# A scaled copy on ScalarE in place of a VectorE product in a chunked scan (one Trainium2 core)

## The reference

```python
proj = hidden_states @ in_proj_w.T
gate, xBC, dt = split(proj)
xBC = silu(conv4(xBC))                    # x, B, C
dt = softplus(dt + dt_bias)
A = -exp(A_log)
# per head: a linear recurrence over the tokens
#   y[t] = sum over s <= t of  C[t].B[s] * exp(sum of dt*A over s+1..t) * dt[s] * x[s]
y = ssd(x * dt, dt * A, B, C) + D * x
hg = y * silu(gate)
s = rmsnorm(hg) @ out_proj_w.T
x = x + s * silu(experts(xn))
```

## Time and profile before

| | us |
|---|---|
| median of 3 runs | 546.95 (546.5 to 547.79) |
| the profiled execution | 545.88 |
| its span, first to last instruction | 544.1 |
| PE busy in the span | 465.5 (86%) |
| VectorE busy | 398.3 (73%) |
| ScalarE busy | 177.0 (33%) |
| GpSimd busy | 288.1 (53%) |

### The profile page before, as it was taken

One profiled execution on the slowest core, in us unless ns is written; L12 is line 12 of the kernel. 1 busy time (PEld: TensorE's weight loads), 2 busy tenths in 40 slices (PEclk: granted clock), 3 DMA queues, 4 the chain that ended last, 5 costly groups with the idle time before them and its releaser, 6 DMA issues. The chain is left out here.

```text
span 544.1 us, 7366 instructions
## 1 busy us (share of the span) xinstructions
PE 465.5 (86%) x2270; PEld 338.3 (62%) x2271; DVE 398.3 (73%) x880; ACT 177.0 (33%) x385; POOL 288.1 (53%) x263
## 2 busy tenths in 40 slices
PE   1786677779998999988889999998959999999970
PEld 1772235566877777956576788997426665665650
DVE  5307898999999999998999999996205544544550
ACT  2541632332333323322323323221323434434420
POOL 3100749583678566586265598991025444444440
PEclk9999677987999979999779999987888999999995
DMA  8994210000000000000000000194863232232224
GB/s 273 295 169 53 104 52 1 1 1 11 9 3 11 10 1 10 11 10 11 1 1 11 11 10 12 39 343 155 311 217 106 87 103 81 88 106 78 68 59 173
DMA packets 27176, 42.10 MB, mean 77 GB/s; under 512 B 2980, under 2 KB 19880, under 8 KB 26952
## 3 DMA queue, kind: packets, MB, share of 16 engines
q1 hardware_dynamic: 23432, 30.53, 19.3%
q0 software_dynamic: 3712, 11.17, 6.9%
HBM read 31.42 MB, written 14.47 MB: 84 GB/s over the span
## 5 line engine op out<-in xcount | busy, mean ns | idle before, releaser
L494 POOL TENSOR_TENSOR ARENA<-ARENA 128x512 f32<-128x512 f32 x112 | 143.1, 1314 | 3.7 <-issue 2.5
L836 PEld LDWEIGHTS BANK<-ARENA 128*128 128x128 f32 x768 | 95.3, 204 | 12.4 <-DVE ARENA L1145 6.5
L836 PE MATMUL BANK<-ARENA 128*128 128x64 f32 x768 | 95.9, 287 | 6.5 <-DVE ARENA L1145 6.0
L788 PE MATMUL BANK<-ARENA,W_MAIN 128*128 128x512 f32 x160 | 82.5, 664 | 16.0 <-DVE ARENA L1145 12.5
L900 PE MATMUL BANK<-ARENA 128*128 x184 | 84.6, 603 | 1.7 <-ACT ARENA L708 1.6
L956 DVE TENSOR_TENSOR ARENA<-ARENA 128x256 f32<-128x256 f32 (+9 forms) x110 | 66.2, 602 | 3.3
L788 PEld LDWEIGHTS BANK<-ARENA,W_MAIN 128*128 128x128 f32 x160 | 32.1, 212 | 56.0 <-issue 31.0
L900 PEld LDWEIGHTS BANK<-ARENA 128*128 128x128 f32 x184 | 35.4, 194 | 37.3 <-issue 36.3
L1126 DVE SCALAR_TENSOR_TENSOR ARENA<-BANK,CONVC,ARENA 128x511 f32<-128x511 f32 (+2 forms) x72 | 53.4, 745 | 3.3 <-ACT ARENA L623 1.6
L557 POOL DMA_INDIRECT final_rows<-ARENA x23 | 24.4, 1060 | 54.7 <-DVE ARENA L956 54.7
L956 DVE TENSOR_TENSOR BANK<-BANK,ARENA 128x256 f32<-128x256 f32 (+1 forms) x112 | 51.8, 463 | 0.8
(11 more groups left out here) (130 smaller groups left out, 755.7 us busy)
## 6 DMA issues: line engine op xcount, KB each, us to landing
ARENA<-in_w_gate SPq DMA_DIRECT2D x8, 512.0 KB, 8.4
ARENA<-in_w_up SPq DMA_DIRECT2D x8, 512.0 KB, 9.3
ARENA<-in_w_down SPq DMA_DIRECT2D x8, 512.0 KB, 10.2
ARENA<-x_by_expert SPq DMA_DIRECT2D x23, 129.0 KB, 3.2
mixer_rows<-ARENA SPq DMA_DIRECT2D x16, 128.5 KB, 2.0
ARENA<-in_x SPq DMA_DIRECT2D x4, 512.0 KB, 5.7
mixer_rows<-in_x SPq DMA_DIRECT2D x1, 2048.0 KB
out_dram<-final_rows SPq DMA_DIRECT2D x4, 512.0 KB, 6.1
```

Of the source, the lines that this page charges most:

```text
L494: nc.gpsimd.tensor_tensor(out=XS[par][:, slot, :].rearrange("p (a h) -> p a h", a=HD), in0=E2[par][:, slot, :].unsqueeze(1).to_broadcast([ ...
L788: ins = nc.tensor.matmul(bank[:, :], lhsT=W_MAIN[:, k, i * P:(i + 1) * P], rhs=XNT[:, k, t * GW:(t + 1) * GW], start=(k == 0), stop=(k == ...
L836: ins = nc.tensor.matmul(bank[:, at:at + 64], lhsT=XS[par][:, lev - 1, blk * P:(blk + 1) * P], rhs=odd(GM[par][:, lev - 1, :], lev), start ...
```

## The change

The neighbour weights W1 move from VectorE to ScalarE. GpSimd's E2 product takes all eight slots instead of seven (128x512 for 128x448 elements), so that DT is multiplied into the NEXT slot there, and ScalarE scales that slot by GD in `turn`, in place of VectorE's product in `head`. The E2 product is a function of its own, `decays`, and is issued in `head` of its tile: in GpSimd's queue that is ahead of Y and S1 of the tile before, where it used to be behind them. The waits follow.

```diff
-        E2 = [part(XSLOTS * HEADS).rearrange("p (l h) -> p l h", l=XSLOTS) for _ in range(2)]
+        E2 = [part(SLOTS * HEADS).rearrange("p (l h) -> p l h", l=SLOTS) for _ in range(2)]
...
-            def sources(t):
+            def decays(t):
                 par = t % 2
                 if t > 1:
                     pool.wait_ge(x_scaled, (t - 1) * XSLOTS)
+                    pool.wait_ge(w1_ready, t - 1)
                 pool.wait_ge(a_moved, a_of("pair", t - par, 1))
                 nc.gpsimd.tensor_tensor(
-                    out=E2[par], in0=E[:, 0:XSLOTS, par, :],
-                    in1=heads_of(DT, t).unsqueeze(1).to_broadcast([P, XSLOTS, HEADS]), op=ALU.mult).then_inc(e2_ready, 1)
+                    out=E2[par], in0=E[:, :, par, :],
+                    in1=heads_of(DT, t).unsqueeze(1).to_broadcast([P, SLOTS, HEADS]), op=ALU.mult).then_inc(e2_ready, 1)
+
+            def sources(t):
+                par = t % 2
                 pool.wait_ge(e2_ready, t + 1)
...
-                if kind == "head" and t == 0:
-                    sources(0)
+                if kind == "head":
+                    decays(t)
+                    if t == 0:
+                        sources(0)
...
                     if t > 0:
                         act.wait_ge(e2_ready, t)
-                        act.wait_ge(w1_ready, t)
...
                 if kind == "turn":
+                    act.wait_ge(e2_ready, t + 1)
+                    if t > 1:
+                        act.wait_ge(a_moved, a_of("turn", t - 2, 1))
+                    nc.scalar.activation(W1[par].rearrange("p (r h) -> p r h", r=2),
+                                         E2[par][:, NEXT, :].unsqueeze(1).to_broadcast([P, 2, HEADS]), ACT.Copy,
+                                         scale=GD[par][:, 1:2]).then_inc(w1_ready, 1)
...
                 if kind == "mid":
+                    pe.wait_ge(d_moved, d_of("head", t))
                     for lev in range(1, LEVELS):
...
                         dve.wait_ge(w0_ready, t - 1)
+                        dve.wait_ge(w1_ready, t - 1)
...
-                    dve.wait_ge(gd_ready, (t + 1) * 2)
-                    dve.wait_ge(a_moved, a_of("pair", t - par, 1))
-                    nc.vector.scalar_tensor_tensor(
-                        out=W1[par].rearrange("p (r h) -> p r h", r=2),
-                        in0=E[:, NEXT, par, :].unsqueeze(1).to_broadcast([P, 2, HEADS]), scalar=GD[par][:, 1:2],
-                        in1=heads_of(DT, t).unsqueeze(1).to_broadcast([P, 2, HEADS]),
-                        op0=ALU.mult, op1=ALU.mult).then_inc(w1_ready, 1)
```

## The result

| | before | after |
|---|---|---|
| median of the timed runs, us | 547.21 (10 runs, 544.85 to 549.03) | 543.57 (10 runs, 542.88 to 545.44) |
| the profiled execution's span, us | 544.1 | 541.1 |
| VectorE busy in the span, us | 398.3 | 392.9 |
| ScalarE busy | 177.0 | 181.6 |
| GpSimd busy | 288.1 | 289.2 |

The ratio is 0.994, with a 95% interval from 0.9924 to 0.9956: 3.6 us gained. The forecast was 10.35 us, and 543.57 lies outside its range of 532 to 542. Helper lines have moved: L956 is now L969, the taps L1126 are L1139, L1145 is L1158, L1168 is L1182, L1076 is L1089.

The account below looks back on a forecast made before the run. VectorE sets the pace (275.73 of 287.00 us busy in the mixer stage), PE close behind. 11.9 + 1.9 - 1.1 - 2.75 - 0.5 + 0.9 = 10.35 us gained, from 546.95 to 536.6 us; 8-in-10 range 532 to 542.

Parts of the forecast that it names:

- the lock: GpSimd products and VectorE instructions with only SBUF operands take one resource in turns, whole instructions long; BANK operands are free of it.
- The 1.08 us per head: Heads of tiles 2 to 12: each W1 removed from VectorE saves 1.08 us, eleven times, 11.9 us gained.
- The first two heads: Start: PE goes on 0.7 us sooner at the first W1, the second saves 1.15 us; together 1.9 us gained.
- PE's wait for L668's product: Listed sign of a wrong forecast: PE waiting for ScalarE's W1 copy, where no PE wait for W1 was expected.
- E2's new place: Even tiles 2 to 10: HG ends later behind E2 and Y, 0.55 us each, 2.75 us lost; tile 12 nothing.
- Behind the train of tile 6: E2 meets the level product and holds the lock: 1.1 us lost, once; behind tile 2's train there is room.
- PE at tile 4: PE, working all of 134.1 to 154.1 us, cannot follow the savings of heads 3 and 4: about 0.5 us lost.
- The last three tiles: GpSimd's chain, 328.25 to 369.33 us: E2 of tile 13 leaves it, W1's removal by itself worth nothing; 0.9 us gained.
- ScalarE and the eighth slot: 16 ScalarE copies of 0.40 us hidden in idle time; larger E2 takes 1.27 us, 0.14 more each in tiles 14 and 15.
- The lock wait only moves: Rival, chance 0.18: odd tiles lose 1.1 us each, even ones 0.55; 4.3 us gained, 542.7 us.
- PE did not become the bound: Rival, chance 0.12: PE refuses VectorE one head's saving in five tiles, 5 x 1.0 us lost; 541.6 us.
- nothing was slower: Rival, chance 0.03: PE brings each pair 2 us later in even tiles 2 to 12; 2.1 us slower, 549.1 us.

Follow-up runs that it names:

- W1 nowhere: Kernel before with the W1 product left out and PE transposing W0 instead; seven-slot E2 in its old place: 545.68 us, 0.9973; ahead of Y: 541.55 us, 0.9896.
- late first train: Changed kernel with GpSimd's first E2 and train held until VectorE's second block of decay sums (da_ready 2 instead of 1): 540.41 us, ratio 0.9887.
- the two that add to it: Changed kernel, GpSimd's first E2 held for da_ready 2, W0's copy in `turn`: 540.79 us, 0.9889; also with E2 between Y and S1: 541.12 us, 0.9892.

## Why the prediction was wrong, step by step

**The bound.** VectorE was rightly read as the busy engine, but 275.73 us busy is not 275.73 us of work. By a sum over the records, of the SBUF-only instructions' time above what the same shape takes when free, some 58 us of VectorE's busy time before were waiting for the lock, 14 of them in W1 (16 x (1.167-0.29)). After it was some 56, all elsewhere. The sum depends on what is taken as free by a us or two.

**The step that failed** is the one that priced each removed W1 at the full 1.08 us: "Both engines move by nearly the same amount, so the places where trains meet the next level products keep their phase; I count nothing there." The rows confirm 1.2 us for GpSimd at head 6, but 1.2 of a 1.29 us grid is no move of the grid, and VectorE's 0.66 is half a step. Most tiles rounded VectorE back to its old place: the table of heads has eleven at nothing and three at one step. Two versions that leave E2 where it was show that the wait is handed on: with W1 nowhere the level product behind head 8 grows from 0.41 to 1.29 us, and with 8 columns in W1's place these take 0.99 us in the mean and the level product is back at 0.41. Where E2 came late, as ahead of head 8, not even GpSimd moved: S1 began at 229.87, behind a Y product that took 1.74 us as HG held it, and the train at 231.09, where it had been 231.10 (head 8 began at 228.69 and at 228.72). Between head 2 and head 13 the forecast was 7.55 us (11.9-1.1-2.75-0.5); the profiles show 217.4 and 216.1 us before and 214.9 after, 1.3 to 2.5.

**The 1.08 us per head** were too much even without that: behind seven taps, about 0.3 us each, 2.1 in all, went into the wait for ScalarE.

**The first two heads, 1.9 us gained.** Nothing of it is seen: head 2 began 0.5 us later than in the first execution of the kernel before and 2.3 later than in the second. The row that I built on, PE's 4.21 us for W1, was one execution's; the second waited 9.3 us for the same product, and the changed kernel 8.65. What decides is whether the first train falls among VectorE's softplus, which I had costed nowhere. The two executions of the kernel before differ there by as much as the term, so what the change itself does to the start is not shown. That a late first train pays in the changed kernel is shown by the time, 0.994 to 0.9887, 2.9 us, and PE's wait for L668's product, which I had called a sign of being wrong, did appear.

**E2's new place.** Ahead of HG I took 0.55 x 5 = 2.75; the HG group grew by 2.3. The size is right, the places are not: HG took 1.49, 1.06, 1.04 and 1.50 ahead of heads 4, 8, 10 and 12, and 0.68 ahead of 2 and 6, and at tile 12 I had put nothing. Behind the train of tile 6 I took 1.1; the level product there took 1.01 in place of 0.42, 0.59. Nothing at tile 2: right (0.42 at 124.15).

**PE at tile 4, 0.5 us.** The gate's products started 1.45 us behind the head at 155.07, in place of 2.39, so PE and ScalarE gave 0.94 of the gain. The lock took it at the next instruction, 1.30 in place of 0.41.

**The last three tiles, 0.9 us.** From head 13 to the end of the scan it took 47.8 us before, in both executions, and 46.8 after: 1.0 gained, the term's size. Its reason holds too, as far as GpSimd's chain goes. With W1 nowhere and E2 in its old place heads 14 and 15 gain their step as well (39.4 us from head 12 to head 15, for 41.0 before), but the last tile gives it back in the wait of 2.1 us for Y, and from head 13 to the end it is 47.6. So W1's removal by itself is worth next to nothing there, as I had it. E2's move by itself is worth less than that: with W1 still on VectorE the stretch takes 49.5. Only both together shorten it, to 46.8, and to 46.5 without the eighth slot and the copies.

**ScalarE and the eighth slot.** The copies take 387 ns in the median, and in the scan no instruction of VectorE or PE waited for one: right. Still the version without W1 and with seven slots in the same order has 0.9896 against 0.994, some 2.4 us, and with E2 in the old place 0.9973 against 0.998, which is within the intervals. The eighth slot adds 16 x 0.14 = 2.2 us to GpSimd, which I had counted only where it cost anything in the last tiles. That the 2.4 us are these 2.2 is not shown: the copies, their waits and the start are not told apart from the slot by any run (in its one profile the version without W1 began head 2 at 109.59 us, 2.2 ahead of the changed kernel, as the second execution of the kernel before did).

**The rivals.** "The lock wait only moves" gave 542.7 us and is the one that came true in kind and nearly in size. The size is partly luck. Its condition was E2 behind the train, and that is not the cause: with E2 in its old place the level products are held as long, and the gain is smaller still. Nor did its sign appear, level products of over 1 us behind the trains of tiles 2 and 6 alike: at tile 2 it is 0.42. The page of the Trainium skill that it drew on (SBUF — State Buffer, section "SBUF: two separate sides") says that the later one waits for the whole instruction of the other; the 8 columns at 986 ns agree. PE did not become the bound, and nothing was slower.

**Where the 3.6 us come from.** The product's removal alone gives 1.3 to 1.5 us, the order alone costs 5.6, both together give 5.5 (0.9896); the changed kernel, with the eighth slot and the copies, keeps 3.6, and 6.0 once its first train starts late. That the order pays only without W1 is shown. Why is shown in one place, the last tile, which is 1.3 us shorter with E2 ahead (22.8 for 24.1 with W1 nowhere) as VectorE waits less for Y. Elsewhere I can only argue: with E2 out of its way each train ends one product sooner, and fewer of the later level and softplus instructions meet it; head to head, the tiles between heads 2 and 3 and between 11 and 12 are 0.7 and 1.1 us shorter than with E2 in place.

## What to carry to other kernels

Before counting a removed instruction at its measured duration, ask how much of that duration is waiting for something that its follower needs as well; an instruction that costs 1.17 us at 128 columns and 0.99 at 8 is worth only what its follower can start and end sooner. Where two engines hand a lock back and forth in a train of equal instructions, time moved in steps of one of these (here 1.27 us): a saving below a step was mostly lost, and one that passed a boundary gave more than itself. And look at what meets at the start of the program: there one more line, the late first train, gave nearly as much again as the change (540.41 us, 0.9887), which makes that version the best of those run, level with the two that add to it. Last, profile the kernel before twice: a wait of 4.21 us in one execution, 9.3 in the next, is no base for a term.

## What was not expected of the hardware

A VectorE product of 8 columns took 986 ns in the mean beside GpSimd, and three products of 128 columns 3.92 us in place of 0.94. And the same removal gives 0.06 us behind head 13 and 1.15 and 1.14 us behind heads 14 and 15, three tiles of the same form (4.20, 5.28 and 5.27 us before, 4.14, 4.13 and 4.13 after). With 8 columns in W1's place, which end only 0.1 to 0.2 us sooner than the 128, the first level products behind heads 14 and 15 already take 0.41 instead of 1.36 and 1.35 us: a tenth of a microsecond decides over a whole step.
